# Row products with 128 stationary columns, and the next attention's weights split in eight pieces

## What is computed

```python
def reference(x, ctx_512, ...):
    ...
    x = _layernorm(x + _L0_attn_ref(x, L0_attn_emb_weight, L0_attn_qkv_w, L0_attn_o_w), axis=-1)
    x = _layernorm(x + _L0_xattn_ref(x, ctx_512, ...), axis=-1)
    x = _layernorm(x + _L0_ffn_ref(x, ...), axis=-1)
    return x
```

```python
qkv = x @ qkv_w.T
...
scores = jnp.einsum('bhqd,bhkd->bhqk', q, k) * scale + bias
attn = jax.nn.softmax(scores, axis=-1)
a = jnp.einsum('bhqk,bhkd->bhqd', attn, v)
...
return a @ o_w.T
```

## Time and profile before

| | us |
|---|---|
| median of 3 runs | 1225.09 |
| lowest, highest | 1222.77, 1226.12 |
| the profiled execution | 1221.6 |
| its span on the core | 1219.8 |

### The profile page before, as it was taken

One profiled execution on the slowest core, in us unless ns is written; L12 is line 12 of the kernel. 1 busy time (PEld: TensorE's weight loads), 2 busy tenths in 40 slices (PEclk: granted clock), 3 DMA queues, 4 the chain that ended last, 5 costly groups with the idle time before them and its releaser, 6 DMA issues.

```text
span 1219.8 us, 24610 instructions
## 1 busy us (share of the span) xinstructions
PE 1145.7 (94%) x8357; PEld 511.2 (42%) x8357; DVE 902.2 (74%) x2849; ACT 809.1 (66%) x1512; POOL 562.4 (46%) x564
## 2 busy tenths in 40 slices
PE   5799999999999999987999999989988999999998
PEld 2333334444444444424422223222223466666666
DVE  2577777777777777775978988998994767656564
ACT  4466666666666666674477887787776866756663
POOL 0987777887777777784423332523211140000000
PEclk9899999999999999998989999999998999999999
DMA  6634332423333333202312222212102522424200
GB/s 204 178 102 126 95 105 76 117 82 84 84 84 84 84 84 82 71 2 66 88 47 62 71 62 64 65 48 79 45 27 80 189 80 69 156 70 153 72 19 18
DMA packets 81570, 102.86 MB, mean 84 GB/s; under 512 B 11842, under 2 KB 73026, under 8 KB 81446
## 3 DMA queue, kind: packets, MB, share of 16 engines
q1 hardware_dynamic: 81030, 100.77, 28.2%
q10 hardware_dynamic: 416, 0.53, 0.2%
HBM read 65.27 MB, written 10.68 MB: 62 GB/s over the span
## 4 chain that ended last, share of the span: by engine, by line
PE 78%; DVE 8%; ACT 6%; issue 6%; ACTq 1%; DMA 1%; POOL 0%; SPq 0%; DVEq 0%; POOLq 0%
PE a_s L1458 10%; PE a_o L499 10%; PE a_m L1444 7%; PE a_a L442 7%; PE a_o L1377 6%; PE a_s L489 5%; PE a_s L490 4%; PE a_m L1333 4%; PE a_e L548 4%; PE a_a L452 4%; DVE a_mx L1793 3%; PE a_m L465 3%; PE a_s L1357 3%; PE a_a L169 3%; PE a_s L1444 2%
## 5 line engine op out<-in xcount | busy, mean ns | idle before, releaser
L1598 ACT ACTIVATE a_pt<-a_s 128x512 f32<-128x512 f32 (+1 forms) x448 | 228.2, 572 | 75.1 <-PE a_s L1357 65.4
L698 ACT ACTIVATE a_pt<-a_s 128x512 f32<-128x512 f32 x256 | 149.5, 597 | 166.3 <-DVE a_s L846 148.2
L1793 DVE TENSOR_REDUCE a_mx<-a_m 128x1 f32<-128x512 f32 x256 | 163.0, 683 | 24.9 <-PE a_m L1333 24.7
L837 DVE CUSTOM_DVE_ANT_0 a_junk<-a_m,a_rtile 128x512 f16<-128x512 f32 x256 | 167.2, 686 | 7.0 <-issue 7.0
L942 POOL TENSOR_TENSOR a_ps<-a_ps,a_pt 128x512 f32<-128x512 f32 x126 | 157.5, 1271 | 0.1
L499 PE MATMUL a_o<-a_pt,a_v 128*64 128x512 f32 x512 | 138.1, 617 | 2.6 <-DVE a_a L851 2.5
L2027 POOL TENSOR_SCALAR_AFFINE_SELECT a_pt<-a_pt 128x512 f32<-128x512 f32 x64 | 40.6, 634 | 205.9 <-ACT a_pt L1598 205.8
L1790 DVE CUSTOM_DVE_ANT_0 a_junk<-a_m,a_causal 128x512 f16<-128x512 f32 (+3 forms) x256 | 113.7, 485 | 9.0 <-issue 8.9
L846 DVE TENSOR_TENSOR a_s<-a_s,a_near 128x218 f32<-128x218 f32 (+1 forms) x256 | 106.6, 431 | 16.2 <-PE a_s L490 14.0
L826 DVE TENSOR_TENSOR a_nat<-a_a,a_nat 128x512 f16<-128x512 f32 x64 | 44.2, 691 | 90.5 <-ACT a_nat L670 90.5
L489 PE MATMUL a_s<-a_q,a_k 128*128 128x512 f16 x256 | 99.0, 387 | 7.0 <-issue 2.9
(11 more groups left out here) (313 smaller groups left out, 2608.1 us busy)
## 6 DMA issues: line engine op xcount, KB each, us to landing
a_rtile<-lines SPq DMA_DIRECT2D x32, 448.0 KB, 3.9
a_q<-a_nat SPq DMA_DIRECT2D x192, 64.0 KB
a_k<-a_nat SPq DMA_DIRECT2D x192, 64.0 KB
a_vy<-in_Wa SPq DMA_DIRECT2D x12, 1024.0 KB, 5.1
a_vy<-in_Wb SPq DMA_DIRECT2D x12, 1024.0 KB, 7.5
a_qk<-halves SPq DMA_DIRECT2D x40, 128.0 KB, 2.8
halves<-a_held SPq DMA_DIRECT2D x16, 256.0 KB, 2.2
halves<-a_held SPq DMA_DIRECT2D x32, 128.0 KB, 2.4
```

Source lines behind the costliest of these rows:

```text
L698: act.activation(pt[:, n % RING, ::-1], bank_s[j % 2][:, :], ACT.Exp, scale=SC1 / QS).then_inc(sm["act_s"], 1)
L837: dve.tensor_tensor_reduce(junk[h][:, :], bank_m[h][:, :], rtile[:, u % 3, h, qb * P:qb * P + S], -1 / MAXROW, 3e38, ALU.add, ALU.min, mx[ ...
L1598: act.activation(to, frm, ACT.Exp, scale=SC2 / QS).then_inc(sm["act_s"], 1)
L1793: dve.tensor_reduce(mx[u % 2][:, qb, to:to + 1], frm, AX.X, ALU.max).then_inc(sm["dve_b"], 1)
```

## The change

The row products load 128 columns in place of 2. For this `mx` becomes 134 columns wide in place of 8; the eight maxima stand in its first eight columns as before, and columns 8 to 133 are set to zero once, by GpSimd, at the start. The product for block qb loads the 128 columns from column 2·qb on, so that its first two are the maxima of that block, and writes all 128 rows of its part of `bank_a`; ACT reads rows 0 and 1, as before. PE waits for the zeros once.

The split of the next attention's weights is made in eight pieces of 320 columns in place of two of 1280, in slots 6, 7, 8, 9, 11, 12, 13 and 14 in place of 6 and 10, at the same point of the slot. The loads stay two, of 1280 columns each; the second is issued at unit 9 in place of 8, and the load of the context at unit 14 in place of 12.

```diff
-        mx = [sb(f"mx{p}", [P, NT, 2], F16) for p in range(2)]
+        MX_W = P + 2 * (NT - 1)
+        mx = [sb(f"mx{p}", [P, MX_W], F16) for p in range(2)]
...
+        W2_LOADS, W2_PIECES = 2, 8
+        W2_LOAD, W2_PIECE, W2_EACH = W2 // W2_LOADS, W2 // W2_PIECES, W2_PIECES // W2_LOADS
+        W2_CUTS = [slice(i * W2_PIECE, (i + 1) * W2_PIECE) for i in range(W2_PIECES)]
+        W2_SLOTS = (6, 7, 8, 9, 11, 12, 13, 14)
...
-                if u == 8:
-                    sp.wait_ge(sm["w2_lo"], 1)
-                    sp.dma_start(w2_raw, io["w2"][:, W2_CUTS[1]]).then_inc(sm["w2_in"], DMA)
-                if u == 12:
-                    sp.wait_ge(sm["w2_lo"], 2)
+                if u == 9:
+                    sp.wait_ge(sm["w2_lo"], W2_EACH)
+                    sp.dma_start(w2_raw, io["w2"][:, W2_LOAD:]).then_inc(sm["w2_in"], DMA)
+                if u == 14:
+                    sp.wait_ge(sm["w2_lo"], W2_PIECES)
...
                 if u == 0:
                     pe.wait_ge(sm["ld_id16"], DMA)
+                    pe.wait_ge(sm["ones"], 3)
                 for qb in range(NT):
-                    mm = pe.matmul(bank_a[0:2, qb * P:(qb + 1) * P], mx[u % 2][:, qb, :], second.ident16[:, :], start=True, stop=True)
+                    mm = pe.matmul(bank_a[:, qb * P:(qb + 1) * P], mx[u % 2][:, 2 * qb:2 * qb + P], second.ident16[:, :], start=True, stop=True)
...
-                    if t in (6, 10) and i == 1:
-                        split_w2(t // 10)
+                    if t in W2_SLOTS and i == 1:
+                        split_w2(W2_SLOTS.index(t))
...
         def gpsimd(pool):
+            for p in range(2):
+                pool.memset(mx[p][:, 2 * NT:], 0.0).then_inc(sm["ones"], 1)
             pool.memset(ones[:, :], WS).then_inc(sm["ones"], 1)
```

More of the change, by code:

```diff
@@ L273, in attention_1 @@
         norm = second.norm
-        W2_CUTS = [slice(i * (W2 // 2), (i + 1) * (W2 // 2)) for i in range(2)]
-        w2_raw = wost[:, :, :].rearrange("p a c -> p (a c)")[:, 0:W2 // 2]
+        W2_LOADS, W2_PIECES = 2, 8
+        W2_LOAD, W2_PIECE, W2_EACH = W2 // W2_LOADS, W2 // W2_PIECES, W2_PIECES // W2_LOADS
+        W2_CUTS = [slice(i * W2_PIECE, (i + 1) * W2_PIECE) for i in range(W2_PIECES)]
+        W2_SLOTS = (6, 7, 8, 9, 11, 12, 13, 14)
+        w2_raw = wost[:, :, :].rearrange("p a c -> p (a c)")[:, 0:W2_LOAD]
+        w2_pieces = [w2_raw[:, W2_CUTS[i]] for i in range(W2_EACH)]
         craw = wost[:, :, :].rearrange("p a (t c) -> p (a t) c", c=CC)
@@ L392, in sync @@
                     sp.wait_ge(sm["wob"], 2)
-                    sp.dma_start(w2_raw, io["w2"][:, W2_CUTS[0]]).then_inc(sm["w2_in"], DMA)
-                if u == 8:
-                    sp.wait_ge(sm["w2_lo"], 1)
-                    sp.dma_start(w2_raw, io["w2"][:, W2_CUTS[1]]).then_inc(sm["w2_in"], DMA)
-                if u == 12:
-                    sp.wait_ge(sm["w2_lo"], 2)
+                    sp.dma_start(w2_raw, io["w2"][:, 0:W2_LOAD]).then_inc(sm["w2_in"], DMA)
+                if u == 9:
[3 more added lines that the diff above has]
+                    sp.wait_ge(sm["w2_lo"], W2_PIECES)
                     sp.dma_start(craw, io["ctx"].rearrange("b (t p) c -> p (b t) c", p=P)).then_inc(sm["ld_ctx"], DMA)
@@ L517, in sums @@
                 if u == 0:
-                    pe.wait_ge(sm["ones"], 1)
+                    pe.wait_ge(sm["ones"], 3)
                     turned.done(pe)
@@ L628, in split_w2 @@
             def split_w2(n):
-                act.wait_ge(sm["w2_in"], DMA * (n + 1))
-                act.activation(second.whi[:, W2_CUTS[n]], w2_raw, ACT.Copy, scale=WS).then_inc(sm["w2_hi"], 1)
+                act.wait_ge(sm["w2_in"], DMA * (n // W2_EACH + 1))
+                act.activation(second.whi[:, W2_CUTS[n]], w2_pieces[n % W2_EACH], ACT.Copy, scale=WS).then_inc(sm["w2_hi"], 1)
             def bridge(e):
@@ L778, in split_w2 @@
                 dve.wait_ge(sm["w2_hi"], n + 1)
-                dve.scalar_tensor_tensor(second.wlo[:, W2_CUTS[n]], w2_raw, WS, second.whi[:, W2_CUTS[n]], ALU.mult, ALU.subtract
+                dve.scalar_tensor_tensor(second.wlo[:, W2_CUTS[n]], w2_pieces[n % W2_EACH], WS, second.whi[:, W2_CUTS[n]], ALU.mult, ALU.subtract
                                          ).then_inc(sm["w2_lo"], 1)
@@ L837, in maximum @@
                     dve.tensor_tensor_reduce(junk[h][:, :], bank_m[h][:, :], rtile[:, u % 3, h, qb * P:qb * P + S], -1 / MAXROW,
-                                             3e38, ALU.add, ALU.min, mx[u % 2][:, qb, h:h + 1]).then_inc(sm["dve_b"], 1)
+                                             3e38, ALU.add, ALU.min, mx[u % 2][:, j:j + 1]).then_inc(sm["dve_b"], 1)
             def add_bias(u, j):
```

## The result

| | before | after |
|---|---|---|
| median of 17 runs | 1220.84 us (1218.83 to 1226.12) | 1217.01 us (1211.96 to 1221.19) |
| after / before | | 0.9965, 95% interval 0.9954 to 0.9976 |
| profiled execution, its span | 1221.6 us, 1219.8 us | 1215.58 us, 1213.8 us |

The 17 runs of before include the three that were known first. The change makes the kernel faster by 0.35% (0.24 to 0.46%): about 4.3 us by the ratio and 3.8 by the medians, where 4.6 us were forecast.

A forecast was written before the change was run, and what follows sets the result against it. TensorE, busy 94% of the span, was taken to bound the kernel through its own issue or waits. Row products 3.6 us plus split 1.0 made 4.6 off 1225.1: 1220.5 us, range 1217.4 to 1224.2.

The forecast's parts named there:

- The base: Whole kernel: the forecast median starts from 1225.1 us, 3.5 us above the profiled execution, less 4.6 us.
- Row products: PE's row products: two gaps of 0.09 us vanish with 128 columns, 0.19 us in 19 ordinary slots, 3.6 us gained.
- Rival A: Row products: the gaps come from semaphore waits, so only the split gains; 1224.1 us, chance 0.09.
- The wider load: Row products' weight loads: 97 ns in place of 82, hidden behind the product before, so costing nothing.
- Rival D: Row products: 128-column loads aren't hidden and each product waits, 9.3 us lost against 4.6; 1229.8 us, chance 0.05.
- slot behind statistics: Eight slots begun right after layer-norm statistics on DVE: PE waits for ACT's copy, so they gain nothing, staying at 15.66 us.
- Spare on ACT: ACT's copy of the rows in ordinary slots: 0.24 us to spare, 0.05 left after the 0.19 gain.
- rival B: Ordinary slots: spare is smaller or a PE wait on DVE replaces it, half of 3.6 us goes; 1222.3 us, chance 0.09.
- The split: Next attention's weights: eight pieces at 0.41 us each, 3.3 us in place of 4.3, so 1.0 us gained.
- DVE before the piece: DVE ahead of its split piece: idle time near nothing, where it waited 0.64 us for ACT before.
- rival C: Split: ACT's piece is late and DVE waits as now, 1.05 us a piece, 8.4 us in all; 1225.6 us, chance 0.05.
- Where PE loses it: PE in the eight split slots: most of the 0.41 us lost at L452 and none at L499.

The follow-up runs named there:

- rows128: The kernel before with only the row products changed, to 128 stationary columns, the split left in two pieces: 1217.27 us, ratio 0.9969.
- rows32: The kernel before with 32 stationary columns in the row products in place of 2: 1220.73 us in one run.
- rows96: The kernel before with 96 stationary columns in the row products in place of 2: 1222.36 us in one run.
- stats: The changed kernel with only the layer-norm statistics moved to DVE's idle place in quarter 1: 1208.24 us, ratio 0.9904 to the kernel before.
- pieces4: The changed kernel with the split in four pieces of 640 columns, in slots 6, 8, 11 and 13: 1216.97 us in one run.
- rows64: The kernel before with 64 stationary columns in the row products in place of 2: 1220.12 us in one run.

## Why the prediction was nearly right on the change and wrong on the time

- **The base: this step failed.** The sum was made against the profiled execution, 1221.6 - 4.6 = 1217.0, and then moved up by 3.5 us, since the median of the three known runs stood at 1225.09. Seventeen runs of the same kernel give 1220.84, and the fourteen without those three 1220.15: the profiled execution was typical, and the three were high. Left where the sum put it, the forecast would have met the measured 1217.01; to the last tenth that would have been luck, since 1221.6 is 0.8 above the median of 17 and 4.6 is 0.8 above the difference of the medians. The range gave this base half of the three runs' distance (1.7 us) and 1.0 for the clock at its lower end, while the stretch up to slot 4 alone lies between 73.4 and 79.5 us in the profiled executions and "the rest" between 686.8 and 690.9; so its lower end was 0.4 us too high.
- **Row products, 3.6 us forecast, 3.7 measured (3.5 in rows128).** Both gaps vanished together, in every ordinary slot by 0.19 to 0.20, and it is the width of the product that decides, as rows32 to rows96 show. Rival A is refuted.
- **The wider load, nothing forecast, nothing measured.** Four products keep their 0.055 us with loads of 97 ns, and with loads of 123. Rival D is refuted. Its own sum was off besides: for a slot behind statistics it took PE's slack of about 0.15 us off the 0.39 and not the 0.19 that the gaps give back there too, so its 1.9 us for these eight slots should have been near 0.4.
- **Spare on ACT, 0.05 us left: held.** In the ordinary slot of after the copy ends at 311.41 and L495 starts at 311.56, 0.15 us later against the 0.10 where ACT is waited for. Ordinary slots gained the whole 0.19; rival B is refuted. Slots behind statistics gained nothing, and stats shows that the statistics' place is why.
- **The split, 4.3 to 3.3 forecast, 4.33 to 3.47 measured.** A piece costs 0.36 where 0.41 was taken, which is the lower bound; ACT moved L722 no more for 320 columns than for the 256 of the earlier trace rows. Seven slots bore this out. The eighth, slot 11, cost 0.95: the bias instruction stands directly behind the piece there and is pushed into GpSimd's addition. This term was missing. That the sum came out so near is luck: the two misses nearly cancel (8 x 0.41 = 3.3 against 3.47).
- **DVE before the piece:** no idle time, as forecast, so rival C is refuted at 320 columns; at 640 it begins to be true (pieces4).
- **Where PE loses it:** forecast was most at L452 and none at L499, which are L457 and L505 in after. Measured in slot 6 are 0.28 us at L457, some 0.08 in the last quarter at L495, and none at L505.
- **Not in the forecast:** single stalls of 0.12 to 0.30 us in one slot of a kernel. Slot 8 has one in before and in rows128, rows32, rows64 and rows96 (0.12); slot 23 has one in every kernel with eight pieces (0.30), whatever else is changed; pieces4 has them in slots 8, 13 and 30. In slot 23 of after, ACT is what starts late:

```profile
379.86 0.60 ACT L704 ACTIVATE a_pt<-a_s 128x512 f32<-128x512 f32 x1 [1.52 <-DVE a_s L852]
```

DVE's L852 (`378.98 0.48`) had ended at 379.46, 0.40 us earlier; in other slots 0.1 us passes. Slots of one kernel are the same work, and the stall's slot changes with the kernel. Its cause stays open: no run tells it apart.

## What to carry to other kernels

A group of small matmuls between full ones paid about 0.09 us on each side here when they loaded 64 stationary columns or fewer, and nothing with 96 or 128, even where the added columns were zeros; so padding is worth a try where the load stays covered and the results' space is free. Work that has to be done anyway costs by its place: cutting it smaller at a place on the path is nearly an exchange (0.9 us), while moving it to where its engine idles takes its price away altogether (3.5 us). Make a sum and its base from the same execution, and take the scatter of the base from where it arises, here the stretches ahead of and behind the one that was changed: three runs didn't hold it.

## What the runs showed of the hardware

- Going from full products to a group with 2, 32 or 64 stationary columns and back cost 0.09 to 0.10 us each way; with 96 or 128 columns it cost nothing. A gap of the same size stands in after ahead of a product with 64 rows (`306.09` to `306.40`, 0.31 where full products follow each other in 0.22), three times a slot. Whether padding to more rows closes it wasn't tried:

```profile
306.09 0.38 PE L496 MATMUL a_s<-a_q,a_k 74*128 74x512 f16 x1
306.40 0.39 PE L470 MATMUL a_m<-a_nat 64*128 64x512 f16 x2
```

- The length of a weight load of the row products grew by about 13 ns for each 32 columns up to 96 and was shorter again at 128: 82 ns for 2 columns, 96 for 32, 109 for 64, 123 for 96, 97 for 128. Neither 123 nor 97 moved the products apart.
- An 8-column `tensor_scalar` on DVE lasts 0.16 us alone, and 0.41 and 0.69 us when it starts while GpSimd's `tensor_tensor` runs: it ends within 0.03 us of it. GpSimd's addition of 0.73 us lasts 0.84 beside a DVE piece of 320 columns and 1.37 beside one of 640.
- TensorE's granted clock between 900 and 1000 us differed between executions (0.93 to 0.98), and the stretch behind slot 33 was the shorter the higher it was, by 4 us from end to end.
